# Degree rows gathered into freed edge slots and added to the node sum by an identity product

## The chip, the cores and the metric

The kernel is one program on one core of a Trainium2 chip. A core has five engines with their own instruction streams, which wait for each other by semaphores: TensorE (PE, matrix products into PSUM), VectorE (DVE), ScalarE (ACT), GpSimd (POOL) and SyncE (SP). SP, ACT and POOL also issue transfers, which 16 DMA engines carry out. The metric is the device time of one execution in microseconds (us); less is better.

## The reference

The input is a graph of 6250 nodes with 256 features each and 100000 edges with 128 features each. The layer adds a graph term and a linear attention term to the nodes, and then a mixture of eight experts with two experts per node. What matters here is the graph term:

```python
in_deg  = minimum(segment_sum(ones, dst), 511)
out_deg = minimum(segment_sum(ones, src), 511)
sum3d   = segment_sum(edge_attr @ W_sum + b_sum, src)
gnn     = xn + z_in[in_deg] + z_out[out_deg] + cent_term + vor_term + sum3d
x = x + gnn + mix(xn)                 # xn is the normalised x
x = x + experts(layernorm(x))         # top 2 of 8, H = 1024
```

So each node takes one row of 256 numbers from the table z_in and one from z_out, chosen by its two degrees. Everything is float32.

## The kernel before

Nodes are cut into 49 tiles of 128 (TILES); a tile is 128 partitions by 256 numbers, and all 49 stay in SBUF in the tensor `state`. Edges are cut into 782 columns of 128. The program has these stages.

1. Sorting and side work (to about 1127 us). SP loads edge rows, ten columns at a time, into a ring of five slots (`X`, named `edge_rows` in the profile, 5 x 10 x 129 numbers per partition). POOL writes each column by an indirect DMA to its sorted place in DRAM (`pool_scatter`, L1725). Beside it the other engines count degrees, compute the attention term and the terms of the nodes, and add them to `state` (`vector_rest`, L1288, which counts `rest_added`).
2. Visits. The sorted edges are read back in blocks, and one-hot products sum them for each tile of nodes into `acc`. A batch of four visits is on DVE one subtraction (L1072), one comparison of 128x1024 numbers (L1077) and four additions (L1065), and on PE eight products (L608). The last visits end at about 1243 us. When the scatters are over, the ring of edge slots is free but for four small arrays at its start.
3. Degree rows. After its last scatter POOL runs `pool_z` for steps 0 to 51. Step t issues the gather of z_in for tile t, and the gather of z_out for tile t - 3 (ZLAG). Both are indirect DMAs with `compute_op=ALU.add`: they add the gathered row into `state` itself (`pool_degrees`, L1759). Gather z_in(t) waits for `rest_added`, z_out(t) for the landing of z_in(t), and z_in(t) also for z_out(t - 6), since six semaphores `z_added` go round (ZRING).
4. Node loop (`tensor_nodes`, `vector_nodes`, `scalar_nodes`, 58 ticks), from the end of the visits on. For tile t PE makes `acc` x `wsum` into a PSUM bank (L788). DVE waits for that product (`n_proj`) and for both degree rows (`z_added`), and adds the bank to `state` (L1315, which counts `n_state`). Five tiles behind PE transposes the normalised tile (L780), seven behind it makes the router's logits (L771); DVE has seven more instructions for each tile, ACT four. PE may make product t once tile t - 2 is added, as there are two banks.
5. Routing (from L1341 on) and experts (from L1787 on): gathers of tokens, eight experts' products in float16 in three terms (L830, L844), and scatter-adds into the result (L1798).

Each engine executes its stream in the order that the program gives it, and there is no scheduler. DMAs that POOL issues are one queue.

Of the kernel before, what the change touches and what calls it, by code (L numbers as in the profile page):

```python
# [10 lines left out]
P = 128  # L11
NODES, DIM, EDGES, EDIM = 6250, 256, 100000, 128
# [50 lines left out]
START = 14  # L63
WEVERY = 5
ZRING, ZLAG = 6, 3
BIGN = TILES * DIM + 48

SLOT = 256
# [104 lines left out]
def build_layer(nc, x, src, dst, edge_attr, vor, cent, z_in, z_out, w_cent, b_cent, w_vor, b_vor,  # L173
# [89 lines left out]
    def late(n):  # L263

        late_at[0] += n
        return edge_mem[:, late_at[0] - n:late_at[0]]
# [108 lines left out]
    xh = part(HR * DIM).bitcast(F16).rearrange("p (r i n) -> p r i n", r=HR, i=2)  # L375
    mv2 = late(2 * TILES).rearrange("p (t i) -> p t i", i=2)
    r1, r2 = late(TILES), late(TILES)
    ps_s, ps_y, ps_log = banks[2:4], banks[5:7], banks[7]


# [127 lines left out]
    def x_free(e, n):  # L508

        if n >= XRING:  # L510
            e.wait_ge(scattered[n % XRING], 16 * LOAD * (n // XRING))

    def part_sorted(e, q):

# [251 lines left out]
    def tensor_nodes(e, tick):  # L766
# [16 lines left out]
        if 0 <= t < TILES:  # L783
            if t == 0:
                e.wait_ge(acc_added, VISITS)
            if t >= 2:
                e.wait_ge(n_state, t - 1)
            e.matmul(ps_s[t % 2][:, 0:DIM], acc[:, t * P:(t + 1) * P], wsum, start=True, stop=True).then_inc(n_proj, 1)  # L788

    def tensor_route(e):  # L790
        e.wait_ge(routed, ROUTE_CHOSEN)
# [498 lines left out]
    def vector_nodes(e, tick):  # L1290
# [20 lines left out]
        if 0 <= t < TILES:  # L1311
            st = state[:, t, :]
            e.wait_ge(n_proj, t + 1)
            e.wait_ge(z_added[t % ZRING], 32 * (t // ZRING + 1))
            e.tensor_tensor(st, st, ps_s[t % 2][:, 0:DIM], ALU.add).then_inc(n_state, 1)  # L1315
        t = tick - 4
        if 0 <= t < TILES:
# [436 lines left out]
        for c in range(LOADS * LOAD, ETILES):  # L1754
            pool_scatter(e, c, XL[:, c - LOADS * LOAD, :], scattered[LOADS % XRING], last_row)

    def pool_degrees(e, i, t):
        table = (z_in, z_out)[i]
        e.indirect_dma_start(state[:, t, :], None, table, bass.IndirectOffsetOnAxis(ap=deg_i[:, i, t:t + 1], axis=0),  # L1759
                             bounds_check=DEG - 1, oob_is_err=True, compute_op=ALU.add).then_inc(z_added[t % ZRING], 16)  # L1760

    def pool_z(e, step):
        t = step
        if t < TILES:
            if t == 0:
                e.wait_ge(deg_done, 3)
            e.wait_ge(rest_added, t + 1)
            if t >= ZRING:
                e.wait_ge(z_added[t % ZRING], 32 * (t // ZRING))
            pool_degrees(e, 0, t)  # L1770
        t = step - ZLAG
        if 0 <= t < TILES:
            e.wait_ge(z_added[t % ZRING], 32 * (t // ZRING) + 16)
            pool_degrees(e, 1, t)

    def pool_gather(e, j):
        if j >= BLOCKS:
# [300 lines left out]
```

## Time and profile before

| | us |
|---|---|
| runs, median of 3 | 2031.07 (2030.84 to 2040.11) |
| the profiled execution | 2035.25 |
| its span | 2033.5 |
| PE busy | 1617.6 |
| DVE busy | 1482.0 |
| POOL busy | 1359.2 |
| ACT busy | 672.7 |

The span is the time from the first to the last instruction of the profiled execution. Busy times are sums over the whole span, and the stages above have different limits, so they do not say which engine a stage waits for; that is read from the rows of the stage. An indirect DMA on POOL is busy only while POOL prepares it; the transfer itself comes after, and the view of one line gives the time from issue to landing.

### The profile page before, as it was taken

To read this page: it belongs to the slowest core of one execution; us is meant where nothing else is said; L and a number is where in the kernel's file an instruction comes from. 1 tells how busy PE (TensorE), PEld (TensorE's weight loads), DVE (VectorE), ACT (ScalarE), POOL (GpSimd) and SP (SyncE) were. 2 spreads that over 40 slices of the span, in tenths; PEclk is the share of its full clock that TensorE was granted. 3 is DMA by queue.
4 is the path that set the end of the run, shared out by engine and by line. 5 is a ranking of instruction groups with operands and counts; after the bars stand their busy time and mean duration, and the time that the engine had idled before them with its cause. 6 is when DMAs were issued, how large, how long until landed. Compare 5 with 4: busy or idle time off the path is not lost. (4 is left out here: it accounts for less than half of the span.)

```text
span 2033.5 us, 38723 instructions
## 1 busy us (share of the span) xinstructions
PE 1617.6 (80%) x12552; PEld 1275.3 (63%) x12552; DVE 1482.0 (73%) x3547; ACT 672.7 (33%) x1486; POOL 1359.2 (67%) x1185
## 2 busy tenths in 40 slices
PE   5555543777888887999977777756899999999997
PEld 1121222344555556889876666646798989889896
DVE  6789888866686756666688888879666666666664
ACT  0001111344333434555510003534444344444342
POOL 5778888777777777777777888840354554554442
PEclk9766755798998998999999999657899999999999
DMA  6378777634454545899998996663499999999995
GB/s 184 92 237 248 219 226 221 188 101 130 126 139 124 141 120 140 234 237 237 254 296 242 236 238 123 130 161 114 150 271 266 263 278 271 272 279 274 266 257 152
DMA packets 381288, 413.79 MB, mean 203 GB/s; under 512 B 46438, under 2 KB 297630, under 8 KB 381086
## 3 DMA queue, kind: packets, MB, share of 16 engines
q1 hardware_dynamic: 192328, 192.74, 30.8%
q10 hardware_dynamic: 129462, 126.47, 23.0%
q0 software_dynamic: 59296, 92.09, 18.5%
q8 instruction: 101, 1.65, 0.3%
q14 instruction: 101, 0.83, 0.1%
HBM read 315.53 MB, written 95.62 MB: 202 GB/s over the span
## 5 line engine op out<-in xcount | busy, mean ns | idle before, releaser
L1725 POOL DMA_INDIRECT sorted_rows<-edge_rows,sorted_pos x780 | 851.7, 1092 | 239.1 <-issue 214.1
L1798 POOL DMA_INDIRECT result<-mixw,edge_rows x105 | 169.6, 1615 | 273.3 <-DVE mixw L1475 189.8
L1680 ACT ACTIVATE mixw<-bank,edge_rows 128x256 f32<-128x256 f32 (+1 forms) x456 | 242.4, 549 | 321.4 <-PE bank L830 227.7
L830 PE MATMUL bank<-edge_rows,big 128*128 128x256 f16 (+1 forms) x2736 | 287.8, 264 | 0.0
L844 PE MATMUL bank<-big 128*128 128x256 f16 x2520 | 284.4, 273 | 1.0 <-issue 1.0
L830 PEld LDWEIGHTS bank<-edge_rows,big 128*128 128x128 f16 x2736 | 248.9, 97 | 30.7
L844 PEld LDWEIGHTS bank<-big 128*128 128x128 f16 x2520 | 244.3, 98 | 28.4 <-issue 1.3
L712 PE MATMUL bank<-mixw,xnT 128*128 128x512 f32 x392 | 200.2, 658 | 66.4 <-ACT xnT L1572 66.1
L608 PE MATMUL bank<-big 128*128 128x128 f32 x1680 | 211.6, 280 | 38.0 <-DVE big L1077 38.0
L1065 DVE TENSOR_TENSOR big<-big,bank 128x128 f32 x588 | 168.6, 287 | 84.4 <-PE bank L608 18.5
L608 PEld LDWEIGHTS bank<-big 128*128 128x128 f32 x1680 | 197.7, 193 | 48.0 <-DVE big L1077 47.6
L1787 POOL DMA_INDIRECT state<-xn_rows,edge_rows x105 | 114.3, 1089 | 122.2 <-DVE edge_rows L1434 90.5
L1077 DVE TENSOR_TENSOR big<-iota,big 128x1024 f32<-128x1024 f32 x147 | 180.1, 1225 | 5.1
L712 PEld LDWEIGHTS bank<-mixw,xnT 128*128 128x128 f32 x392 | 77.2, 207 | 154.7 <-issue 81.9
L1461 DVE SCALAR_TENSOR_TENSOR big<-mixw,edge_rows,big 128x512 f16<-128x512 f32 (+1 forms) x228 | 161.8, 710 | 8.1
L1459 DVE TENSOR_SCALAR big<-mixw,edge_rows 128x512 f16<-128x512 f32 (+1 forms) x228 | 106.9, 469 | 64.0 <-ACT mixw L1680 60.1
L1472 DVE SCALAR_TENSOR_TENSOR mixw<-bank,edge_rows 128x256 f32<-128x256 f32 x105 | 50.8, 484 | 119.8 <-PE bank L844 119.6
L1614 ACT ACTIVATE mixw<-mixw,sig_cols 128x128 f32<-128x128 f32 x196 | 80.8, 483 | 89.6 <-issue 56.4
L1759 POOL DMA_INDIRECT state<-L_gnn_z_in,deg_i x49 | 96.3, 1964 | 14.9 <-issue 14.0
L1759 POOL DMA_INDIRECT state<-L_gnn_z_out,deg_i x49 | 94.3, 1924 | 14.9 <-issue 13.7
L587 PE MATMUL bank<-sort_hot,rank_matrix 128*128 128x500 bf16 (+1 forms) x79 | 37.6, 476 | 82.0 <-DVE sort_top L1038 72.2
L608 PE MATMUL bank<-big,mixw 128*128 128x128 f32 x672 | 84.3, 279 | 19.2 <-DVE big L1077 19.2
(328 smaller groups left out, 2631.6 us busy)
## 6 DMA issues: line engine op xcount, KB each, us to landing
big<-w_parts SPq DMA_DIRECT2D x114, 1024.0 KB, 7.1
big<-sorted_rows ACTq DMA_DIRECT2D x420, 129.0 KB
edge_rows<-edge_attr SPq DMA_DIRECT2D x78, 640.0 KB
mixw<-sorted_rows ACTq DMA_DIRECT2D x168, 129.0 KB
big<-L_ffn_W ACTq DMA_DIRECT2D x128, 128.0 KB
w_parts<-big ACTq DMA_DIRECT2D x64, 256.0 KB, 4.3
sorted_rows<-edge_rows,sorted_pos POOLq DMA_INDIRECT x780
edge_rows<-L_ffn_b SPq DMA_DIRECT2D x57, 128.0 KB, 6.4
```

The source lines that it names most:

```text
L608: ins = e.matmul(ps_visit[b % 2][:, i * P:(i + 1) * P], visit_rows[visit_slot(b)[0]][:, i, k, 0:EDIM], visit_hot[:, b % 2, i, k, :], start ...
L712: ins = e.matmul(ps_kv[h], xnT[:, t % 2, k, :], kvw[:, k, h * INNER:(h + 1) * INNER], start=(k == 0), stop=(k == KC - 1))
L830: ins = e.matmul(ps_h[h % 4][:, w], W1r[:, r, a, k, h * P:(h + 1) * P], xT[:, r, b, k, w], start=(k == 0 and s == 0), stop=(k == KC - 1 an ...
L844: ins = e.matmul(ps_o[s][:, 0:DIM], hT[:, r, a, h, s * P:(s + 1) * P], W2r[:, r, b, h, :], start=(h == 0 and i == 0), stop=(h == HC - 1 an ...
L1065: e.tensor_tensor(acc[:, bass.ds(o, P)], acc[:, bass.ds(o, P)], ps_visit[b % 2][:, i * P:(i + 1) * P], ALU.add).then_inc(acc_added, 1)
L1077: e.tensor_tensor(visit_hot[:, b % 2].rearrange("p v k n -> p (v k) n"), iota.unsqueeze(1).to_broadcast([P, n, P]), visit_key[:, b % 2].re ...
L1461: e.scalar_tensor_tensor(lo, hs, m_r[:, n, HC + 1:HC + 2], hi, ALU.mult, ALU.subtract).then_inc(h_parted, 1)
L1680: e.activation(h32[:, h, w], ps_h[h % 4][:, w], ACT.Gelu, bias=m_r[:, n, h:h + 1], scale=m_r[:, n, HC:HC + 1]).then_inc(gelu_done, 1)
L1725: e.indirect_dma_start(sorted_rows, bass.IndirectOffsetOnAxis(ap=row_pos[:, c:c + 1], axis=0), rows, None, bounds_check=last_row, oob_is_e ...
L1759: e.indirect_dma_start(state[:, t, :], None, table, bass.IndirectOffsetOnAxis(ap=deg_i[:, i, t:t + 1], axis=0), bounds_check=DEG - 1, oob_ ...
L1787: e.indirect_dma_start(xg[:, j % XG, h].rearrange("p i k n -> p (i k n)"), None, xn_rows, bass.IndirectOffsetOnAxis(ap=slot_tok[:, s:s + 1 ...
L1798: e.indirect_dma_start(y_rows, bass.IndirectOffsetOnAxis(ap=slot_tok[:, tile:tile + 1], axis=0), yo[:, j % YO, s, :], None, compute_op=ALU ...
```

## The change

The gathers no longer touch `state`. Twenty-four places of 256 numbers (ZROWS) are laid in the ring of edge slots, behind the small arrays that live there (ZAT = 306). z_in(t) is gathered plainly, without an addition, into place (t + 19) mod 24; z_out(t) is gathered with an addition into the same place. PE then adds the place to the node's sum: behind the product with `wsum`, and in the same PSUM accumulation, it multiplies the row with the identity. The wait for the degree rows moves from DVE to PE. z_in(t) no longer waits for `rest_added`; for t below 24 it waits until the edge slots under its place are scattered, from t = 24 on until PE has counted product t - 24, which used the same place.

```diff
+ZROWS = 24
...
+    ZAT = XRING * LOAD * XW - ZROWS * DIM
+    assert late_at[0] <= ZAT
...
+    def z_row(t):
+
+        a = ZAT + (ZROWS - 5 + t) % ZROWS * DIM
+        return edge_mem[:, a:a + DIM]
+
+    def z_slots(t):
+
+        a, w = ZAT + (ZROWS - 5 + t) % ZROWS * DIM, LOAD * XW
+        return range(a // w, (a + DIM - 1) // w + 1)
+
+    def slot_scattered(e, r):
+
+        more = ETILES - LOADS * LOAD if r == LOADS % XRING else 0
+        e.wait_ge(scattered[r], 16 * (LOAD * len(range(r, LOADS, XRING)) + more))
...
@@ tensor_nodes
-            e.matmul(ps_s[t % 2][:, 0:DIM], acc[:, t * P:(t + 1) * P], wsum, start=True, stop=True).then_inc(n_proj, 1)
+            e.matmul(ps_s[t % 2][:, 0:DIM], acc[:, t * P:(t + 1) * P], wsum, start=True, stop=False)
+            e.wait_ge(z_added[t % ZRING], 32 * (t // ZRING + 1))
+            e.matmul(ps_s[t % 2][:, 0:DIM], ident, z_row(t), start=False, stop=True).then_inc(n_proj, 1)
...
@@ vector_nodes
             e.wait_ge(n_proj, t + 1)
-            e.wait_ge(z_added[t % ZRING], 32 * (t // ZRING + 1))
             e.tensor_tensor(st, st, ps_s[t % 2][:, 0:DIM], ALU.add).then_inc(n_state, 1)
...
@@ pool_z
-            e.wait_ge(rest_added, t + 1)
+            if t < ZROWS:
+                for r in z_slots(t):
+                    slot_scattered(e, r)
+            else:
+                e.wait_ge(n_proj, t - ZROWS + 1)
             if t >= ZRING:
                 e.wait_ge(z_added[t % ZRING], 32 * (t // ZRING))
-            pool_degrees(e, 0, t)
+            e.indirect_dma_start(z_row(t), None, z_in, bass.IndirectOffsetOnAxis(ap=deg_i[:, 0, t:t + 1], axis=0),
+                                 bounds_check=DEG - 1, oob_is_err=True).then_inc(z_added[t % ZRING], 16)
         t = step - ZLAG
         if 0 <= t < TILES:
             e.wait_ge(z_added[t % ZRING], 32 * (t // ZRING) + 16)
-            pool_degrees(e, 1, t)
+            e.indirect_dma_start(z_row(t), None, z_out, bass.IndirectOffsetOnAxis(ap=deg_i[:, 1, t:t + 1], axis=0),
+                                 bounds_check=DEG - 1, oob_is_err=True, compute_op=ALU.add).then_inc(z_added[t % ZRING], 16)
```

The order of instructions on POOL is the same; the kind of every other one and its waits change. These rows of POOL's stream, in the degree-row stage, begin with the gather z_in(23) of the kernel before. A row has the line, the operation, what it writes and reads, its size and the semaphores that it waits for:

```order
L1759 DMA state<-L_gnn_z_in,deg_i 128x256 [waits z_added5,rest_added]
L1759 DMA state<-L_gnn_z_out,deg_i 128x256 [waits z_added2]
L1759 DMA state<-L_gnn_z_in,deg_i 128x256 [waits z_added0,rest_added]
L1759 DMA state<-L_gnn_z_out,deg_i 128x256 [waits z_added3]
L1759 DMA state<-L_gnn_z_in,deg_i 128x256 [waits z_added1,rest_added]
```

The same place of POOL's stream in the changed kernel, z_in(23) first:

```order
L1788 DMA edge_rows<-L_gnn_z_in,deg_i 128x256 [waits z_added5,scattered4,scattered3]
L1793 DMA edge_rows<-L_gnn_z_out,deg_i 128x256 [waits z_added2]
L1788 DMA edge_rows<-L_gnn_z_in,deg_i 128x256 [waits z_added0,n_proj]
L1793 DMA edge_rows<-L_gnn_z_out,deg_i 128x256 [waits z_added3]
L1788 DMA edge_rows<-L_gnn_z_in,deg_i 128x256 [waits z_added1,n_proj]
```

The third row is z_in(24), the first gather that reuses a place: it, and the z_out(21) queued behind it, now wait for PE's first node.

On PE one tick of the node loop was, in the kernel before (transposes, product, logits; `mixw` holds the normalised tile, `big` holds `acc`):

```order
L780 MATMUL bank<-ident,mixw 128x128 [waits n_yT,n_y]
L780 MATMUL bank<-ident,mixw 128x128
L788 MATMUL bank<-wsum,big 128x256 [waits n_state]
L771 MATMUL bank<-wr_t,mixw 128x8 [waits n_yT]
L771 MATMUL bank<-wr_t,mixw 128x8
```

In the changed kernel the same tick on PE has one product more, which reads the place in the edge slots:

```order
L798 MATMUL bank<-ident,mixw 128x128 [waits n_yT,n_y]
L798 MATMUL bank<-ident,mixw 128x128
L806 MATMUL bank<-wsum,big 128x256 [waits n_state]
L808 MATMUL bank<-edge_rows,ident 128x256 [waits z_added0]
L789 MATMUL bank<-wr_t,mixw 128x8 [waits n_yT]
L789 MATMUL bank<-wr_t,mixw 128x8
```

The identity product stands between the product and the logits of an older tile, and carries the wait for `z_added` that the addition on DVE had.

## Rows read from the trace of the kernel before

**Rows 1.** Page, chain that ended last: shares of the span by engine.

```profile
PE 31%; POOL 6%; issue 5%; DVE 2%; DMA 2%; POOLq 0%; ACT 0%; DVEq 0%; ACTq 0%
```

**Rows 2.** Line L1759, 1127 to 1244.5 us: count, ns min/median/max, first and last start.

```profile
L1759 POOL DMA_INDIRECT state<-L_gnn_z_in,deg_i x23: 1560/2487/2506, 1127.6 to 1241.4; - x23
L1759 POOL DMA_INDIRECT state<-L_gnn_z_out,deg_i x20: 1560/2487/2487, 1138.1 to 1243.3; - x20
```

**Rows 3.** Line L1759, 1244.9 to 1350 us, with its waits, waiters and landing.

```profile
L1759 POOL DMA_INDIRECT state<-L_gnn_z_out,deg_i x29: 1560/1560/1693, 1247.0 to 1346.1; - x29
L1759 POOL DMA_INDIRECT state<-L_gnn_z_in,deg_i x26: 1560/1560/1653, 1245.1 to 1338.7; - x26
...
  DVE state L1315: 21.2, 11
...
DMA to landing us min/median/max: 3.6/3.9/4.5
```

**Rows 4.** Line L1787 (plain gather, as many bytes a row), 1430 to 1500 us.

```profile
L1787 POOL DMA_INDIRECT state<-xn_rows,edge_rows x19: 1007/1012/1164, 1438.2 to 1490.9; - x19
```

**Rows 5.** Line L1798 (scatter with addition), 1430 to 1500 us.

```profile
L1798 POOL DMA_INDIRECT result<-mixw,edge_rows x8: 1555/1616/1629, 1463.2 to 1498.3; - x8
```

**Rows 6.** Timeline of POOL: start us, us, engine, line, operation [idle before].

```profile
1117.97 0.97 POOL L1725 DMA_INDIRECT sorted_rows<-edge_rows,sorted_pos  x1 [0.30 <-issue]
1119.25 1.21 POOL L1725 DMA_INDIRECT sorted_rows<-edge_rows,sorted_pos  x1 [0.30 <-issue]
...
1140.89 2.49 POOL L1759 DMA_INDIRECT state<-L_gnn_z_in,deg_i  x1 [0.30 <-issue]
1143.68 2.49 POOL L1759 DMA_INDIRECT state<-L_gnn_z_out,deg_i  x1 [0.30 <-issue]
```

**Rows 7.** Timeline of DVE in the visits.

```profile
1118.39 1.23 DVE L1077 TENSOR_TENSOR big<-iota,big 128x1024 f32<-128x1024 f32 x1
...
1121.18 1.23 DVE L1077 TENSOR_TENSOR big<-iota,big 128x1024 f32<-128x1024 f32 x1
...
1140.72 1.23 DVE L1077 TENSOR_TENSOR big<-iota,big 128x1024 f32<-128x1024 f32 x1
```

**Rows 8.** Timeline of PE: the first products, then two neighbours of one tick.

```profile
1243.59 3.47 PE L788 MATMUL bank<-wsum,big 128*128 128x256 f32 x10 [1.82 <-DVE big L1065]
...
1250.38 0.60 PE L788 MATMUL bank<-wsum,big 128*128 128x256 f32 x2
1250.82 0.51 PE L771 MATMUL bank<-wr_t,mixw 128*128 128x8 f32 x4
```

**Rows 9.** Timeline: DVE's additions of tiles 7, 27 and 48, and routing's first.

```profile
1252.41 0.40 DVE L1315 TENSOR_TENSOR state<-state,bank 128x256 f32<-128x256 f32 x1
...
1288.93 0.40 DVE L1315 TENSOR_TENSOR state<-state,bank 128x256 f32<-128x256 f32 x1
...
1350.03 0.40 DVE L1315 TENSOR_TENSOR state<-state,bank 128x256 f32<-128x256 f32 x1
...
1357.99 0.57 DVE L1341 TENSOR_TENSOR mixw<-bank,br_t 128x392 f32<-128x392 f32 x1
```

**Rows 10.** Timeline of PE near the loop's end, granted clock 0.50.

```profile
1347.51 0.67 PE L780 MATMUL bank<-ident,mixw 128*128 128x128 f32 x2
...
1347.97 1.06 PE L788 MATMUL bank<-wsum,big 128*128 128x256 f32 x2
...
1348.82 0.86 PE L771 MATMUL bank<-wr_t,mixw 128*128 128x8 f32 x4
...
1349.53 0.67 PE L780 MATMUL bank<-ident,mixw 128*128 128x128 f32 x2
```

**Rows 11.** Windows: busy us (count) by engine, PEclk, DMA share, GB/s.

```profile
1127.00:1230.00 103.00, 75.62 (x592) 68.57 (x591) 87.18 (x222) 1.28 (x1) 91.65 (x38) 1.00 1.00 238
1244.00:1298.00 54.00, 41.25 (x234) 34.18 (x233) 53.64 (x238) 34.49 (x115) 45.16 (x30) 0.92 0.68 132
1298.00:1350.00 52.00, 33.74 (x129) 29.91 (x128) 30.68 (x129) 19.79 (x64) 41.76 (x27) 0.50 0.62 111
```

More of the change, by code:

```diff
@@ L1755, in pool_last_edges @@
             pool_scatter(e, c, XL[:, c - LOADS * LOAD, :], scattered[LOADS % XRING], last_row)
[L1757 to L1760, printed above, removed]
     def pool_z(e, step):
```

## The prediction

> **What bounds the kernel now.** I read the chain of waits first. By engine it names PE with 31% and POOL with 6% of the span [rows 1]; PE's part is the experts' stage, which the change does not touch, so only the stretch in which POOL is named can move. That is the stretch of the degree rows, and I read POOL's line L1759 there. It starts 43 gathers up to 1244.5 us, 23 of z_in and 20 of z_out [rows 2], and 55 after it, the last at 1346.1 [rows 3]. Between two gathers lie 0.30 us in every timeline row [rows 6], so a gather costs 2.49 + 0.30 = 2.79 us beside the visits and 1.56 + 0.30 = 1.86 us in the node loop: POOL is never free. Then who waits: DVE's addition stands 21.2 us for rows that have not landed [rows 3]. The last addition is at 1350.03, 3.9 us after the last gather's start, which is the time from issue to landing [rows 3, 9]. So POOL's 98 gathers set the end of the node loop, and routing starts 8 us behind it, at 1357.99.
>
> It is not so for the whole loop. From tile 7 to tile 27 DVE takes (1288.93 - 1252.41) / 20 = 1.83 us a tile [rows 9], and it is busy for 53.64 of 54 us [rows 11]: up to about tile 30 DVE is the bound, since POOL had a lead of 20 finished tiles, and POOL only from there, at two gathers or 3.73 us a tile.
>
> **The plain gather.** The trace has no plain gather of these tables. The nearest row is L1787, which gathers 128 rows of the same 1024 bytes without an addition: 1.01 us on POOL [rows 4]. L1798, with an addition, takes at least 1.56 us [rows 5], as L1759 does [rows 3]; the scatter without one takes 0.97 [rows 6]. The addition is what these pairs differ in, so I take 1.01 for z_in. The bounds are 0.97 and 1.56 us. z_out stays at 1.56.
>
> **Beside the visits: almost nothing.** A gather there takes 2.49 us because of DVE's comparison. z_in at 1140.89 starts 0.17 us behind the start of a comparison and ends at 1143.38, which is the comparison's end at 1141.9 plus 1.5 [rows 6, 7]; the next one starts at 1143.68 and meets the next comparison. One gather goes through in each batch of 2.79 us. With one of two at 1.01 us, I place them on that beat: z_in behind a comparison, z_out, z_in again, and only the second z_out starts inside a comparison. That makes four gathers in three batches, 8.4 us for two tiles instead of 11.2. z_in(4) would start at about 1136 and z_in(24) at 1136 + 20 x 4.2 = 1220. But z_in(24) reuses the place of tile 0 and waits for PE's first node, and that cannot be before the last visit: PE's first product starts at 1243.59 [rows 8]. POOL stands about 24 us, with z_out(21) behind it in the queue, and nobody waits for either. So the faster gathers give a lead of 24 and 21 instead of 23 and 20, one tile, and if the beat stays at 2.79 us the lead is just as before. The early start without `rest_added` gives nothing: POOL stands at no wait for it in the first gathers.
>
> The DMA engines show a busy share of 1.00 beside the visits [rows 11], and there will be more rows in that stretch. I cost this at nothing: DVE keeps its 2.79 us there [rows 7], and only two transfers more are issued before the visits end. If visit blocks came late, each microsecond would be one lost.
>
> **In the node loop: the gain.** POOL goes on when PE has done node 0, at 1243.59 + 0.9 = 1244.5. There remain 25 of z_in and 28 of z_out. The last one starts at 1244.5 + 25 x (1.01 + 0.30) + 27 x (1.56 + 0.30) = 1244.5 + 32.8 + 50.2 = 1327.5, against 1346.1: 18.6 us earlier. With z_in at 0.97 it is 19.6, at 1.56 it is 4.9.
>
> DVE must keep up: tile 48 at its own pace is 1252.41 + 41 x 1.83 = 1327.4. The last row lands at 1327.5 + 3.9 = 1331.4, so the rows stay the last by 4 us, from about tile 41 on. If DVE's pace is the end, more of the gathers' gain is useless.
>
> **What PE gets.** 49 identity products of 128x256 float32. The trace has the same shape in L788: 0.60 us alone, and 0.44 from its start to the next instruction's [rows 8]; at half clock 1.06 and 0.85 [rows 10]. At full clock PE is busy 41.25 us for 32 tiles, 1.29 a tile [rows 11], and comes to 1.73, under DVE's 1.83: hidden. At half clock a tile takes 0.46 + 0.85 + 0.71 = 2.02 us by the starts of rows 10, and would take 2.87. In the last stretch, with 3.17 us between rows, that is hidden too, but the last three z_out come 1.86 us apart, so at half clock PE falls behind by 2 x (2.87 - 1.86) = 2.0 us. I take half of that, 1.1. And the last row now passes the identity product before DVE can add it: 0.6 to 1.1 us, I take 1.0. The wait that moved to PE has logits and transposes of older tiles behind it; these were behind DVE's wait too, by way of the normalised tile.
>
> Sum: -18.6 + 1.0 + 1.1 = -16.5 us. Last addition 1333.5; routing and all behind it move as a block, since they start from the last node. The span becomes 2017.0 and the profiled execution's 2035.25 becomes 2018.8. That execution lies 4.2 us above the median of the runs, 2031.07; I forecast against the median: 2014.6 us, written 2014.5.
>
> **Rivals.** *Half clock (the slower side).* The granted clock is full beside the visits, 0.92 on average in 1244 to 1298, and 0.50 from there on [rows 11]. Were it half through the whole loop, PE at 2.87 us a tile would be the bound: 1244.5 + 48 x 2.87 + 1.3 = 1383.6, 33.5 us later than now: 2064.6. It decides from (1350.0 - 1244.5) / 48 = 2.20 us a tile on, which is 17 of 48 tiles at half clock. For it: PE is not quickly back at full clock, 0.50 held to the end. Against it: the same clock stayed full beside the visits with PE busy 75.62 of 103 us, and PE now has a third more to do in each tile. With the 0.92 of before, 8 tiles at half clock cost 8 x 1.04 = 8 us on DVE's 1327.4, that is 4 us net: 2018.5, inside my own range.
> The Trainium skill, page "TensorE: Matmul & The Clock Gate", section "HAM oscillation — how this bites in real kernels", says that a PE which waits for transfers between short pieces of work drops to half clock each time; the rows at 0.50, all in the stretch that waits for degree rows, agree, and by that rule alone half clock belongs to the last tiles, which have room for it.
>
> *The plain gather is no cheaper.* If the 0.55 us belong to the table gather and not to the addition, 25 x 0.55 = 13.8 us are gone and the change gives 2.7: 2028.4. Rows 4 and 5 speak against it, but they are other tensors.
>
> *POOL holds DVE in the visits.* z_out of 1.56 us now sometimes starts before a comparison and runs into it. If the comparison then waited for it, up to 1.2 us in each 8.4 us between 1136 and 1220, the visits would end 10 x 1.2 = 12 us later: 2026.5. Against it: the scatter of 1117.97 ran until 1118.94 over the start of the comparison at 1118.39, and the next comparison still came 2.79 us later [rows 6, 7].
> The Trainium skill, page "SBUF — State Buffer", section "Who interferes with whom", says that whoever starts first keeps the shared port for its whole instruction and that issue order decides who blocks; by it this rival would happen, and also before with the scatters. The trace agrees for POOL behind a comparison and not for DVE behind a scatter, so I go by the rows, with 2014.5 instead of 2026.5.
>
> **How the numbers follow.** My forecast, 2009 to 2021 with the bounds of the gather's price, DVE's pace and some half clock: 0.66. Better than that: 0.04. Half clock in more tiles: 0.17, of which 0.08 ends above 2041. No cheaper gather: 0.08. DVE held: 0.05. The range 2009 to 2030 leaves out the 0.04 below and about 0.12 of the half clock. A measurement can tell about 0.5% from no change, 10.2 us. Faster by more than that, below 2020.9: 0.66 + 0.04 + 0.02 of mild half clock, 0.72. Within: 0.07 of half clock, 0.08 and 0.05, 0.20. Slower: 0.08.
>
> **What would show it.** Right: z_in near 1.01 us in the node loop; a stand of POOL at its 25th z_in until about 1244.5; the last z_out at 1327 to 1328; DVE's last addition at 1332 to 1335; routing about 16 us earlier; comparisons on a beat of 2.79 us. Wrong: z_in at 1.56; PE without a gap at a clock of 0.5 before tile 41; a longer beat in the visits; or a routing stage that takes back what the loop gave.

## The result, and the profile after

The change takes 2017.59 us (median of 5 runs, 2012.65 to 2020.65) where the kernel before took 2035.31 (median of its 5 runs, 2030.84 to 2040.11): a ratio of 0.9912 [0.9895, 0.9929], or 17.7 us less, with an interval of 14.5 to 21.4. The profiled execution took 2020.65 us and its span is 2018.9, against 2035.25 and 2033.5: 14.6 us less in the span. The prediction had 2014.5 us and 16.5 us less.

The page, first the busy time of the engines and then the chain that ended last by engine:

```profile
PE 1623.6 (80%) x12650; PEld 1277.8 (63%) x12650; DVE 1477.1 (73%) x3547; ACT 669.8 (33%) x1486; POOL 1305.3 (65%) x1185
...
PE 49%; DVE 12%; issue 5%; ACTq 5%; ACT 3%; DMA 2%; DVEq 1%; POOL 1%; SPq 0%; POOLq 0%
```

POOL had 6% of the chain [rows 1] and has 1%. (The other shares can't be compared: the shares of [rows 1] add up to 46% of the span and these to 78%, so this chain could be followed further back.) POOL's busy time fell from 1359.2 to 1305.3 us. PE has 98 instructions more, two for each identity product.

The view of the plain gather's line before the node loop, then from 1244.5 us on (count, ns min/median/max, first and last start, then what POOL waited for):

```profile
L1788 POOL DMA_INDIRECT edge_rows<-L_gnn_z_in,deg_i x24: 1012/1031/1967, 1125.9 to 1205.0; - x24
...
L1788 POOL DMA_INDIRECT edge_rows<-L_gnn_z_in,deg_i x25: 1024/1028/1082, 1245.4 to 1322.3; - x25
...
  PE bank L808: 39.3, 10
```

And of the gather with addition, the same two stretches, with its landing in the second:

```profile
L1793 POOL DMA_INDIRECT edge_rows<-L_gnn_z_out,deg_i x21: 1547/1554/2581, 1131.5 to 1207.3; - x21
...
L1793 POOL DMA_INDIRECT edge_rows<-L_gnn_z_out,deg_i x28: 1547/1552/1653, 1246.8 to 1329.2; - x28
...
DMA to landing us min/median/max: 3.6/3.8/4.8
```

These answer to [rows 2, 3]. In the loop z_in costs 1.03 us in place of 1.56, and z_out takes 1.55. The lead at the start of the loop is 24 and 21 gathers instead of 23 and 20, and the last gather starts at 1329.2 instead of 1346.1.

POOL's timeline, a stretch beside the visits and the stand in front of the loop, and then DVE's comparisons in the first stretch:

```profile
1157.48 2.28 POOL L1793 DMA_INDIRECT edge_rows<-L_gnn_z_out,deg_i  x1 [0.30 <-issue]
1160.07 1.96 POOL L1788 DMA_INDIRECT edge_rows<-L_gnn_z_in,deg_i  x1 [0.31 <-DMA edge_rows<-L_gnn_z_out,deg_i]
1162.34 1.55 POOL L1793 DMA_INDIRECT edge_rows<-L_gnn_z_out,deg_i  x1 [0.30 <-issue]
1164.19 1.03 POOL L1788 DMA_INDIRECT edge_rows<-L_gnn_z_in,deg_i  x1 [0.30 <-issue]
1165.52 1.55 POOL L1793 DMA_INDIRECT edge_rows<-L_gnn_z_out,deg_i  x1 [0.30 <-issue]
1167.38 1.03 POOL L1788 DMA_INDIRECT edge_rows<-L_gnn_z_in,deg_i  x1 [0.30 <-DMA edge_rows<-L_gnn_z_out,deg_i]
1168.71 2.28 POOL L1793 DMA_INDIRECT edge_rows<-L_gnn_z_out,deg_i  x1 [0.30 <-issue]
...
1207.28 1.55 POOL L1793 DMA_INDIRECT edge_rows<-L_gnn_z_out,deg_i  x1 [0.31 <-issue]
1245.43 1.03 POOL L1788 DMA_INDIRECT edge_rows<-L_gnn_z_in,deg_i  x1 [36.59 <-PE bank L808]
```

```profile
1157.11 1.22 DVE L1097 TENSOR_TENSOR big<-iota,big 128x1024 f32<-128x1024 f32 x1
1159.90 1.23 DVE L1097 TENSOR_TENSOR big<-iota,big 128x1024 f32<-128x1024 f32 x1
1162.69 1.23 DVE L1097 TENSOR_TENSOR big<-iota,big 128x1024 f32<-128x1024 f32 x1
1165.49 1.29 DVE L1097 TENSOR_TENSOR big<-iota,big 128x1024 f32<-128x1024 f32 x1
1168.35 1.22 DVE L1097 TENSOR_TENSOR big<-iota,big 128x1024 f32<-128x1024 f32 x1
```

The pattern comes back after 11.23 us, from 1157.48 to 1168.71: six gathers, three tiles, in four batches of the visits, 3.74 us a tile where [rows 6] had two batches of 2.79 us. The z_out of 1157.48 starts 0.37 us behind the start of a comparison and takes 2.28 us, the z_in of 1160.07 starts 0.17 us behind one and takes 1.96. The z_out of 1162.34 starts 0.35 us ahead of one, and neither is longer for it. The z_out of 1165.52 starts 0.03 us behind one: it takes its own 1.55 us, and the comparison takes 1.29 us in place of 1.23. Then POOL stands 36.59 us, until PE has counted node 0, although it has work left.

DVE's last additions and routing's first instruction on its timeline, then two of PE's identity products in the stretch at half clock:

```profile
1333.76 0.41 DVE L1334 TENSOR_TENSOR state<-state,bank 128x256 f32<-128x256 f32 x1
...
1341.74 0.57 DVE L1360 TENSOR_TENSOR mixw<-bank,br_t 128x392 f32<-128x392 f32 x1
```

```profile
1314.55 1.22 PE L808 MATMUL bank<-edge_rows,ident 128*128 128x256 f32 x2
...
1317.85 1.22 PE L808 MATMUL bank<-edge_rows,ident 128*128 128x256 f32 x2
```

Against [rows 9] the last addition is 16.27 us earlier and routing 16.25: the block moved as one, up to there. The windows of [rows 11], with the end of the loop at 1334, and a short one inside it (busy us and count by engine, granted clock, DMA share, GB/s):

```profile
1127.00:1230.00 103.00, 75.41 (x589) 68.56 (x590) 87.15 (x223) 1.28 (x1) 68.50 (x44) 1.00 0.93 247
1244.00:1298.00 54.00, 50.91 (x305) 44.20 (x304) 53.30 (x239) 33.42 (x116) 42.54 (x33) 1.00 0.61 140
1298.00:1334.00 36.00, 32.14 (x154) 25.03 (x154) 28.61 (x128) 19.65 (x65) 27.05 (x20) 0.81 0.60 136
1316.00:1322.00 6.00, 5.95 (x19) 4.26 (x19) 3.50 (x16) 2.29 (x8) 5.08 (x4) 0.50 0.58 131
```

Beside the visits DVE is as busy as before, 87.15 us against 87.18. In the first 54 us of the loop PE is busy for 9.7 us more and the clock is full. The half clock that held from 1298 to 1350 is now a piece within 1298 to 1334 (0.50 in the window of 1316). There the identity products come 3.30 us apart, which is the rows' pace and not PE's: [rows 10] and one product more make 2.87 us a tile at this clock, and POOL's timeline in the same stretch has no gap above 0.31 us. (PE shows 5.95 us busy of 6.00 all the same: shown times take in waits. The identity product is shown for 1.22 us here, and for 1.06 at this clock where it doesn't wait, in e0 below.)

```profile
1312.74 1.03 POOL L1788 DMA_INDIRECT edge_rows<-L_gnn_z_in,deg_i  x1 [0.30 <-PE bank L808]
1314.07 1.55 POOL L1793 DMA_INDIRECT edge_rows<-L_gnn_z_out,deg_i  x1 [0.30 <-issue]
1315.93 1.03 POOL L1788 DMA_INDIRECT edge_rows<-L_gnn_z_in,deg_i  x1 [0.30 <-PE bank L808]
```

The gap "until PE bank L808" is the usual one; the product was done before POOL came to it. From 1245.43 on the 53 gathers follow each other without a stand.

### The profile page after: what moved, and what is told of

It reads as the page before. It is cut to its first block, busy times and chain, and to the rows that moved or that the text cites. A ratio compares the mean times of both kernels' runs of the same rounds, so it can differ in the third digit from the quotient of the medians.

```text
span 2018.9 us, 38870 instructions
## 1 busy us (share of the span) xinstructions
PE 1623.6 (80%) x12650; PEld 1277.8 (63%) x12650; DVE 1477.1 (73%) x3547; ACT 669.8 (33%) x1486; POOL 1305.3 (65%) x1185
## 4 chain that ended last, share of the span: by engine, by line
PE 49%; DVE 12%; issue 5%; ACTq 5%; ACT 3%; DMA 2%; DVEq 1%; POOL 1%; SPq 0%; POOLq 0%
PE bank L850 14%; PE bank L864 13%; PE bank L626 6%; PE bank L730 6%; ACTq L1885 3%; DVE big L1097 3%; DVE big L1085 2%; PE bank L764 1%; PE bank L819 1%; PE bank L708 1%; PE bank L821 1%; PE bank L836 1%; PE bank L773 1%; ACT mixw L1633 1%; ACTq L1973 1%
## 5 line engine op out<-in xcount | busy, mean ns | idle before, releaser
L1117 DVE TENSOR_TENSOR hotA<-iotab,dst_h 128x500 bf16<-128x500 bf16 (+1 forms) x79 | 33.0, 417 | 89.4 <-PE bank L641 88.9
L626 PEld LDWEIGHTS bank<-big,mixw 128*128 128x128 f32 x672 | 78.1, 192 | 24.3 <-DVE big L1097 24.3
```

Source lines behind the costliest of these rows:

```text
L626: ins = e.matmul(ps_visit[b % 2][:, i * P:(i + 1) * P], visit_rows[visit_slot(b)[0]][:, i, k, 0:EDIM], visit_hot[:, b % 2, i, k, :], start ...
```

## The experiments

Four chips were used. On the first and the fourth the visits end at about 1243 us. On the second and third they end some 600 us later, and the kernel before takes 2629.26 us (median of 28 runs, 2613.57 to 2645.76) on the second and 2611.9 and 2619.88 (two runs) on the third. So I read, beside the whole time, the **loop**: from DVE's first addition to its last. On the first chip it is 105.7 us before (1244.3 to 1350.0) and 89.1 after (1244.7 to 1333.8), that is 16.6 us less. Where there is only one run of a kernel, only the loop is used. For some I also give the **tail**, from the start of the last z_out to the last addition. It is 3.9 us before and 4.5 after on the first chip.

### Second chip: the change again, the addition back, fewer places, six gathers past the places

**e0_change_again** is the changed kernel with no edit.

> The change itself once more, on the same chip as the others: 0.990 to 0.993 of the kernel before; last addition at 1333 to 1335 us, POOL's stand 35 to 37 us. It is the measure for the two others of which a few microseconds are asked.

Measured: 2637.98 us (12 runs) against 2629.26, ratio 1.0033 [1.0008, 1.0058], so 8.7 us slower where 0.990 to 0.993 was expected. The loop takes 92.3 us (1857.1 to 1949.4). The view of the plain gather's line:

```profile
L1788 POOL DMA_INDIRECT edge_rows<-L_gnn_z_in,deg_i x49: 1015/1032/2054, 1424.4 to 1934.8; - x49
...
  PE bank L808: 358.2, 9
  DVE deg_i L1122: 181.9, 1
```

The degree rows begin at 1424 us, the visits end at about 1857. POOL fills its 24 places and then stands most of 358.2 us in front of the loop. The lead is the same 24 and 21 gathers as on the first chip, however long POOL has. The kernel before has no such limit; what it does with the time was seen on the third chip, below.

The loop is 3.2 us longer than on the first chip, and nearly all of that is the tail: 7.6 us, at a granted clock of 0.50 from about 1923 to 1947. POOL's last z_out, two of PE's products with `wsum` behind it, and DVE's last addition:

```profile
1941.74 1.56 POOL L1793 DMA_INDIRECT edge_rows<-L_gnn_z_out,deg_i  x1 [0.30 <-issue]
...
1942.76 1.06 PE L806 MATMUL bank<-wsum,big 128*128 128x256 f32 x2
...
1945.64 1.06 PE L806 MATMUL bank<-wsum,big 128*128 128x256 f32 x2
...
1949.35 0.40 DVE L1334 TENSOR_TENSOR state<-state,bank 128x256 f32<-128x256 f32 x1
```

At half clock PE takes 2.88 us a tile, and the last rows come 1.87 us apart, so PE falls behind them.

**e1_zin_adds** gives z_in its addition back, in the places. It then adds to what a place still holds, so its sums are not the reference's.

```diff
             e.indirect_dma_start(z_row(t), None, z_in, ...,
-                                 bounds_check=DEG - 1, oob_is_err=True).then_inc(...)
+                                 bounds_check=DEG - 1, oob_is_err=True, compute_op=ALU.add).then_inc(...)
```

> The change with z_in gathered with an addition again, into the same places (the sums are then not the reference's). Theory, the price of the plain gather is the gain: z_in takes 1.56 us on POOL instead of 1.03. POOL still stands at z_in(24) until about 1245.4 us; the last z_out starts at 1245.4 + 25 x 1.86 + 27 x 1.86 = 1342 and DVE's last addition is at 1346 to 1347, 13 us later than in the change (1333.8). Time about 2031, 13 us over the change. Rival, the gain came from the places in the edge ring, the early start or the wait that left DVE: the last addition stays at 1334 and the time near 2017.

Measured: 2650.9 us (9 runs), ratio 1.0082 [1.0053, 1.0111]. z_in takes 1.56 us again:

```profile
L1788 POOL DMA_INDIRECT edge_rows<-L_gnn_z_in,deg_i x49: 1558/1560/2587, 1410.4 to 1936.0; - x49
```

The loop takes 106.5 us, 14.2 more than with the plain gather, and the whole time is 12.9 us more than e0's, as expected. The 25 gathers inside it cost 25 x (1.56 - 1.03) = 13.3 us more. So the addition is what the plain gather saves, and POOL's queue in the loop is where it is saved.

**e2_16_places** lays 16 places instead of 24.

```diff
-ZROWS = 24
+ZROWS = 16
```

> The change with 16 places instead of 24. Theory, the number of places is POOL's lead when the node loop starts, and each place is worth one z_in and one z_out in the loop, 1.33 + 1.86 = 3.19 us: 33 z_in and 36 z_out remain at 1245.4, the last z_out starts at 1245.4 + 33 x 1.33 + 35 x 1.86 = 1354.4, last addition at 1358 to 1359, 25 us later than in the change. Rival, DVE's or PE's pace in the loop sets the end and the lead has slack: last addition at most 3 us later, 1337.

Measured: one run; the loop takes 115.9 us (1851.8 to 1967.7), 23.6 more than with 24 places, or 2.95 us for each place. A tile costs POOL 1.03 + 1.56 + 2 x 0.30 = 3.19 us, so eight tiles of lead are 25.5 us, as expected. The lead at the start of the loop is a term of its own, as large as the price of a gather.

**e4_six_direct** uses the time in which POOL stands: z_in and z_out of tiles 24 to 29 are gather-added into `state`, as in the kernel before, and need no place; the later tiles use places again.

```diff
+ZDIRECT = 6
...
         if 0 <= t < TILES:
             if t < ZROWS: ...
+            elif z_direct(t):
+                e.wait_ge(rest_added, t + 1)
             else:
-                e.wait_ge(n_proj, t - ZROWS + 1)
+                e.wait_ge(n_proj, z_place(t) - ZROWS + 1)
...
-            e.indirect_dma_start(z_row(t), None, z_in, ...)
+            e.indirect_dma_start(z_row(t), None, z_in, ...,
+                                 compute_op=ALU.add if z_direct(t) else ALU.bypass)
```

(`z_row(t)` is `state[:, t, :]` for these six, PE leaves their identity product out, and DVE waits for `z_added` before it adds them.)

> The change, but tiles 24 to 29 take both rows by an addition straight into the state, as before the change, so that POOL uses its stand of 36.6 us for 12 more gathers at 2.79 us; the tiles after them use the 24 places again. Theory, POOL's lead is what holds the end back: the last z_out starts at about 1245.4 + 19 x 1.33 + 21 x 1.86 = 1310, nobody waits for rows any more, and DVE's own pace of 1.75 to 1.83 us a tile sets the last addition at 1253.0 + 41 x 1.78 = 1326 to 1328, 6 to 7 us earlier than in the change. Time 2010 to 2012 where the change has 2017. Rival, PE is already the bound with 1.7 us a tile, or the routing stage takes it back: last addition or time as in the change.

Measured: 2631.11 us (12 runs), ratio 1.0006 [0.9977, 1.0035]; the loop takes 81.6 us. That is 10.7 us less than e0's, where 6 to 7 were expected. (The whole times in the expectation are for a chip like the first.) Its window:

```profile
1861.40:1943.00 81.60, 73.56 (x446) 63.40 (x444) 81.46 (x365) 52.01 (x180) 54.11 (x41) 1.00 0.57 133
```

DVE is busy for 81.46 of 81.60 us: with six tiles more of lead the gathers no longer show, and the loop is DVE's, 1.78 us a tile from tile 7 to tile 27 and 1.74 at the end. The loss on this chip is gone, but nothing is gained on the kernel before.

### Third chip: the kernel before again, no identity product, two of them, all in `state`

**b0_before_again** is the kernel before with no edit.

> The kernel before, once more with a profile, because on the chip of the last runs the sorting and the visits end about 600 us later than in the first profile (node loop from 1857 instead of 1244 us), and the change was 1.0033 of the kernel before there. Theory: POOL's lead decides. With late visits the kernel before has issued all 98 gathers before the loop starts (98 x 2.79 = 273 us, and over 400 us were there), the loop then runs at DVE's pace and takes 82 to 84 us from the first to the last addition, while the change stands at its 24th place and takes 92; that is the 9 us. With early visits, as in the first profile, it takes 105 to 106 us. Rival, the change loses elsewhere (routing, experts, visits): the loop of the kernel before takes over 92 us with late visits too.

Measured: the loop takes 82.2 us (1845.3 to 1927.5), as expected. The view of the gathers' line:

```profile
L1759 POOL DMA_INDIRECT state<-L_gnn_z_in,deg_i x49: 1557/1559/1627, 1405.6 to 1629.1; - x49
L1759 POOL DMA_INDIRECT state<-L_gnn_z_out,deg_i x49: 1560/1831/2589, 1419.9 to 1638.6; - x49
...
  DVE state L1288: 231.6, 20
```

All 98 gathers are out by 1641 us, 204 us before the loop starts, at 1.56 us or more. Here they cost nothing, and the change puts 53 of them back into the loop: 92.3 against 82.2 us, 10.1 more, beside the 8.7 us that the whole time on the second chip shows. (The two loops are from two chips; no chip here ran both kernels with a profile in this schedule.) The wait for `rest_added`, which never held POOL on the first chip, holds it for 231.6 us in 20 gathers here, and costs nothing either.

**e3_no_identity** keeps the gathers as in the change and leaves the identity product out, so the degree rows are missing from the sums; DVE waits for the rows again.

```diff
-            e.matmul(ps_s[t % 2][:, 0:DIM], acc[...], wsum, start=True, stop=False)
-            e.wait_ge(z_added[t % ZRING], 32 * (t // ZRING + 1))
-            e.matmul(ps_s[t % 2][:, 0:DIM], ident, z_row(t), start=False, stop=True).then_inc(n_proj, 1)
+            e.matmul(ps_s[t % 2][:, 0:DIM], acc[...], wsum, start=True, stop=True).then_inc(n_proj, 1)
```

> The change without the identity product; DVE waits for the rows again (the degree rows are then missing from the sums). POOL's stream is that of the change. Theory, the product costs only its own latency behind the last row: the loop from the first to the last addition is 0.5 to 2 us shorter than the change's 89.1 (first chip) or 92.3 (second chip), and the granted clock drops earlier, since PE has less to do. Rival, the product holds the loop up in every tile: at least 4 us shorter.

**e6_identity_twice** makes the identity product twice, which adds the row twice.

```diff
             e.wait_ge(z_added[t % ZRING], 32 * (t // ZRING + 1))
+            e.matmul(ps_s[t % 2][:, 0:DIM], ident, z_row(t), start=False, stop=False)
             e.matmul(ps_s[t % 2][:, 0:DIM], ident, z_row(t), start=False, stop=True).then_inc(n_proj, 1)
```

> The change with the identity product made twice (the degree rows count twice in the sums). Theory, PE has 0.1 us of room in each tile and no more: busy 50.9 of 54 us for 31 tiles is 1.64 a tile, and 0.44 more makes 2.1 against DVE's 1.75 to 1.83, so PE becomes the bound and the loop takes 96 to 102 us instead of 89 to 92. Rival, PE's busy time overstates what it needs, and by its issue times (0.27 + 0.44 x 3 + 0.35 = 1.94 a tile) the loop takes 93 to 95 us; or it is free: 89 to 92.

Measured, loops in the order none, one (the change, second chip), two: 88.5, 92.3, 89.9 us. Their windows, one kernel each:

```profile
1834.30:1922.80 88.50, 74.14 (x359) 62.93 (x358) 81.64 (x365) 52.16 (x179) 69.58 (x53) 0.74 0.63 140
```

```profile
1857.10:1949.40 92.30, 85.71 (x454) 72.42 (x453) 82.41 (x366) 52.61 (x180) 69.63 (x53) 0.87 0.60 135
```

```profile
1839.00:1928.90 89.90, 89.25 (x548) 80.62 (x547) 84.28 (x366) 55.48 (x180) 69.17 (x53) 1.00 0.61 139
```

In all of them POOL's 53 gathers set the pace of the end (69.17 to 69.63 us of busy time and 53 gaps of 0.30). What a product costs is read in the tail: 3.9 us without it, as in the kernel before, and with one 4.5 us (first chip, full clock), 5.6 (the held run on the fourth, below) and 7.6 (second chip, half clock). So one product costs 0.6 to 3.7 us at the end of the loop, and not its 49 x 0.44 = 21.6 us, and how much depends on the granted clock there. That the loop without it is 0.6 to 3.8 us shorter says the same, but across chips and from one run.

With two products the tail is 5.6 us at full clock. What I expected first, a loop of 96 to 102 us, fell, and the last case, 89 to 92 us, held. But the product is not free inside the loop. PE's timeline with two:

```profile
1855.32 0.60 PE L806 MATMUL bank<-wsum,big 128*128 128x256 f32 x2
1855.75 0.59 PE L808 MATMUL bank<-edge_rows,ident 128*128 128x256 f32 x2
1856.19 0.59 PE L809 MATMUL bank<-edge_rows,ident 128*128 128x256 f32 x2
...
1857.23 0.60 PE L806 MATMUL bank<-wsum,big 128*128 128x256 f32 x2
```

PE has no gap and needs 1.91 us a tile, and DVE's additions of tiles 7 to 27 come 1.91 us apart, where they come 1.78 apart with one product and with none. That is the 1.94 us by issue times of the expectation's second case: PE is the bound there. It is hidden because the rows come last: 10.1 us for the first seven tiles and 41 x 1.91 make 88.4 us, just under the measured 89.9. So there was room for one product more, and by this estimate not for two. My error in the first case was to take PE's busy time, 1.64 us a tile at full clock, as what it needs: a product is shown for 0.59 us and the next one starts after 0.43.

The clock in the loop was 0.74, 0.87 and 1.00 with none, one and two, one run each. That the products made the difference is not shown: the kernel of e5, next, has no identity product, and its loop ran at 0.65 here and, with POOL held, at 0.96 on the fourth chip.

**e5_plain_in_state** leaves the places out: z_in is gathered plainly into `state`, over what is there (which is lost, so the sums are not the reference's), and z_out is added to it.

```diff
-            e.indirect_dma_start(z_row(t), None, z_in, ...)
+            e.wait_ge(rest_added, t + 1)
...
+            e.indirect_dma_start(state[:, t, :], None, z_in, ...)
```

> The kernel before with one edit: z_in is gathered plainly into the state, over what stands there (the sums are then not the reference's), z_out is added as before. No places, no identity product. Theory, this has the whole gain of the cheaper gather and no end to the lead: with early visits POOL has about 33 z_in out when the loop starts, the rest ends near 1300 us, and the loop runs at DVE's pace, 82 to 84 us instead of 105.7; z_in takes 1.01 to 1.04 us outside the visits. With late visits, 82 to 84 us as well. Rival, the loop needs the places or PE's addition for its gain: over 88 us.

Measured: the loop takes 85.0 us, 1 above what I expected and 7.3 below the change's on the second chip, with every gather out before it (1394.1 to 1612.7 for z_in, at 1.03 us). It has neither cap nor identity product. It doesn't have all of the clock either, 0.65:

```profile
1829.00:1914.00 85.00, 79.31 (x354) 69.80 (x353) 81.52 (x366) 53.30 (x180) 0.00 (x0) 0.65 0.18 64
```

From about 1848 to 1886, and again from 1895 on, it was 0.50, and the additions of tiles 26 to 30 come 2.03 us apart. That is PE's pace at half clock, 2.02 us a tile by [rows 10]. b0 ran the last 29 us of its loop at 0.50 too, and at 2.03 us a tile. Neither has a gather in its loop. So with the gathers out of the way, PE at half clock is what holds these two loops above DVE's 1.74 to 1.78 us a tile.

### Fourth chip: four kernels with POOL held

All four wait for the same point of the visits before POOL's first z_in. It was meant to give the schedule of the first chip to a chip of any kind.

```diff
             if t == 0:
                 e.wait_ge(deg_done, 3)
+                e.wait_ge(acc_added, VISITS - 168)
```

The fourth chip turned out to be of the early kind (the kernel before: 2034.89 us, 15 runs), so the hold was short, 9.91 us in the first of the four, 3.05 and 3.04 in the next two and none in the last. The runs compare the kernels in one schedule but don't show that the schedule is what differs between chips. The first is the kernel before with the hold, the second the change with it, the third adds ZDIRECT = 6 as above, the fourth is the one with everything in `state`.

> The kernel before with one wait more: POOL may start its first degree gather only when all but 168 of the visits are added, which is 42 batches before the node loop, as it happened by itself in the first profile. It sets the early-visit schedule on any chip. Theory, POOL's lead at the loop's start decides: 23 z_in and 20 z_out are out when the loop starts, and the loop from first to last addition takes 104 to 107 us as in the first profile (105.7), against 82.2 without the hold where visits are late. On such a chip the time is then 21 to 25 us over the kernel before. Rival, what made the loop short there was the chip and not the lead: 82 to 90 us and no change in time.

> The change with the same hold. Theory: it cannot use an earlier start, since its 24 places are full by 1208 of 1244 us in the first profile; so the hold costs nothing, the loop takes 89 to 93 us, and the time is within 2 us of the change without hold. Against the held kernel before it is 13 to 17 us faster, the sign and size of the first chip's result (17.7), although the chip may be another. Rival, the sign belongs to the chip: held, the change is slower than the held kernel before.

> The change with tiles 24 to 29 gathered with additions into the state, and the same hold. Theory: POOL does twelve more gathers at 2.79 us in its stand, the loop is at DVE's pace and takes 81 to 84 us, 6 to 10 us less than the held change; time within 2 us of the kernel before without hold where visits are late, and 21 to 25 us under the held kernel before. Rival, the lead of six tiles is eaten by the slower gathers beside the visits or by waits: over 87 us.

> The kernel before with z_in gathered plainly over the state (its sums are not the reference's), and the same hold. Theory, the cheaper gather alone has the gain, and without places nothing stops the lead: the beat beside the visits is three tiles in four batches, 3.7 us a tile, so about 31 z_in are out when the loop starts, the rest is out some 55 us later, and the loop takes 82 to 85 us. Rival, the places or PE's addition are needed: 95 us or more.

| held kernel | us (runs) | ratio to the kernel before | loop | clock in it |
|---|---|---|---|---|
| before | 2037.97 (10) | 1.001 [0.9989, 1.0031] | 106.2 | 0.59 |
| change | 2023.31 (6) | 0.9938 [0.9918, 0.9958] | 90.2 | 0.91 |
| six direct | 2014.39 (4) | 0.9875 [0.9835, 0.9915] | 80.9 | 1.00 |
| all in `state` | 2010.82 (4) | 0.9877 [0.9833, 0.992] | 80.1 | 0.96 |

The windows of the change and of the third:

```profile
1246.70:1336.90 90.20, 82.97 (x456) 70.32 (x455) 81.66 (x365) 52.84 (x180) 69.55 (x53) 0.91 0.60 138
```

```profile
1250.50:1331.40 80.90, 73.60 (x447) 63.70 (x445) 80.82 (x365) 52.03 (x180) 54.10 (x41) 1.00 0.58 134
```

The change takes 14.7 us off the held kernel before, and 16.0 off its loop, where the first chip had 17.7 and 16.6. Against the kernel before without a hold it is 11.6 us. The six direct tiles take off 8.9 us more and 9.3 of the loop. Twelve gathers of these tiles went out before the loop, so POOL has 41 in the loop's window where it had 53. Those of z_in ran beside the visits at the stretched price, in time that was a stand before:

```profile
L1806 POOL DMA_INDIRECT edge_rows<-L_gnn_z_in,deg_i x43: 1012/1040/1968, 1133.0 to 1309.1; - x43
L1806 POOL DMA_INDIRECT state<-L_gnn_z_in,deg_i x6: 2483/2487/2494, 1216.5 to 1244.4; - x6
```

DVE is busy for 80.82 of 80.90 us. This is the version that beats both kernels: 1.25% under the kernel before on its chip, and 0.44% under the change. (Both were held; the hold made no difference clear of noise to the kernel before, 1.001 [0.9989, 1.0031].) The fourth kernel needs no places and no product, its loop of 80.1 us is 2 us under what I expected, and its time is not clear of the third's, so with the stand filled the gathers have nothing more to give: at 80 us and a clock near full the loop is DVE's, 1.74 to 1.78 us a tile. The kernel with six direct tiles and without the hold was not run on an early chip.

## Why the prediction was right, point by point

**The sum** was -18.6 for the gathers, +1.0 for the product's latency and +1.1 for half clock at the end. Measured in the loop it was -16.9, +0.6 and 0. The mechanism was right and the total of 16.5 us was close partly by luck, as the points on the last z_out and the identity product say. The median came out at 2017.59 and not 2014.5 mostly because the base moved: the kernel before has a median of 2031.07 from three runs and 2035.31 from five.

**The bound** was POOL's gathers in the loop, as read. e1 shows it: 0.53 us on each of 25 gathers gave 14.2 us on the loop.

**The plain gather** at 1.01 us, from a gather of another tensor [rows 4], was 1.03. The rival that it is no cheaper, 2028.4 us, fell.

**Beside the visits** the mechanism was right and two sizes were off. I placed four gathers in three batches, 4.2 us a tile; there were six in four, 3.74 us. In each four batches one z_out starts 0.37 us inside a comparison and takes 2.28 us, and the z_in behind it starts in the next one and takes 1.96; the other four take their own time, though two of them run beside a comparison. I had two stretched gathers in every three batches. z_in(24) was therefore reached at about 1209 instead of 1220, and the stand was 36.6 us, not 24. As the places cap the lead, it changed nothing: one tile of lead, as predicted. What I read wrongly is its worth. "Nobody waits for either" is true of the stand, but e4 and the third held kernel show that the stand holds 9 us of work that could have been done in it.

**POOL holds DVE** (2026.5 us) fell, but not to nothing. In one of four batches a z_out starts 0.03 to 0.04 us behind the comparison, which then takes 1.29 us in place of 1.23, and the next one comes 2.86 us later in place of 2.79. This happened six times, 0.4 us in all: the comparisons ran 0.49 us ahead of those of the kernel before at 1126 us and 0.08 us ahead at 1238. The price I had set for each meeting was 1.2 us. The Trainium skill, page "SBUF — State Buffer", section "Who interferes with whom", says that whoever issues first gets the shared port pair for its whole instruction. It says so of DVE instructions in a mode with two ports; this comparison comes under its line on two inputs in SBUF, and for such instructions the section infers that they don't stop POOL from preparing a DMA. The trace agrees with neither in full. POOL behind a comparison's start does wait: the z_out that starts 0.37 us behind ends 1.43 us after the comparison's end. A gather that starts 0.35 us ahead doesn't hold the comparison (1.23 us), so the measurement decides against the rule in that order.

**The last z_out** was to start at 1327.5 and started at 1329.2. Of the 1.7 us, 0.9 is the later first gather (1245.43, not 1244.5; PE's first product, at 1243.50, was not late) and 25 x 0.02 = 0.5 the price of z_in; the rest is spread over 53 gathers, none of which waited.

**DVE's pace** was taken from before, 1.83 us a tile. It was 1.77: tile 7 was added at 1253.01 and tile 27 at 1288.48. So there was more room beneath the gathers than I had.

**The identity product** was hidden, as predicted. On this chip the 1.1 us for half clock at the end was not needed: the clock was back at full when the last rows came (1.00 from 1328 on), and the last addition is 1333.76, 4.5 us behind the last gather where it was 3.9 [rows 3, 9]. That is 0.6 us, within the 0.6 to 1.1 of the latency alone. The smaller terms cancelled the late z_out: 1333.76 against 1333.5. That the clock came back in time was luck. In e0 it didn't, PE took 2.88 us a tile as I had worked out (2.87), and the tail was 3.7 us over the 3.9, where my two terms are 2.1 together. (Half of the 2.0 us that I had for the falling behind is 1.0, and I wrote 1.1.)

**Half clock as the bound** (2064.6 us) fell: the clock over the loop was 0.71 before and 0.92 after. The argument held against this rival, that PE has a third more to do in each tile, points the right way for this pair; that it is the cause is not shown, as e5 says. The Trainium skill, page "TensorE: Matmul & The Clock Gate", section "HAM oscillation — how this bites in real kernels", says that short pieces of work between waits for transfers drop the clock. The stretch at 0.50 within 1298 to 1334 agrees, where PE's rows come 3.30 us apart. But the prediction says that the rows at 0.50 are all in the stretch that waits for degree rows, and the 0.92 of [rows 11] hides others: 0.61 from 1274 to 1280 and 0.82 from 1280 to 1286, where PE waited for DVE and ACT only, and DVE's first wait for a row is the one before 1303.52. The last 29 us of b0's loop at 0.50 have no gather in them. So waits for transfers are one way to lose the clock here and not the only one.

**Routing and the rest** moved as a block, by 16.25 us. The span fell by 14.6, so 1.6 us of it was given back between routing and the end of this execution, inside the scatter of the runs (2012.65 to 2020.65). Medians give 17.7 us less, the prediction had 16.5.

**What the prediction did not have** is the schedule. It took the place of the degree rows beside the visits as given, and wrote that the early start without `rest_added` gives nothing. On two of four chips they start some 430 us before the loop. There the cap of 24 places is a loss, and the change is slower by 1.0033 [1.0008, 1.0058]. A rival "the cap takes a lead that the old kernel had" could have been worked out from the code and the rows: the change leaves 25 x 1.33 + 28 x 1.86 = 85.3 us of gathers to the loop always, and the kernel before leaves less than that once 98 - 85.3 / 1.86 = 52 gathers are out before it. On the first chip 43 were, on the third all 98.

## What to carry to other kernels

A ring of places between a producer and its consumer sets the largest lead, and the lead at the start of a stage is worth the producer's price for each item (here 3.19 us a tile): count it as a term of its own and ask what it is when the producer comes early. Where a producer stands at a full ring, look for a second place for its results; six of them gave 8.9 us here, on top of the 14.7 of the change. Whether an engine has room for another instruction is read from start to start of its instructions and not from its busy time (0.43 against 0.59 us for a product here), and at the lower clock too: the same product cost 0.6 us at the end of the loop at full clock and up to 3.7 at half.

## What the runs showed of the hardware that was not expected

The same kernel took 2035 us on two chips and 2612 to 2629 on two others. On the second chip DVE's degree step shows waits whose releaser is only "remote", and on the first the same line has none. Of the other two chips the late one has such waits (422.5 us in 45 in the kernel before) and the early one none in this line. The line's view on the second chip, 200 to 1700 us:

```profile
L1117 DVE TENSOR_TENSOR hotA<-iotab,dst_h x79: 211/420/422, 891.4 to 1417.1; 128x500 bf16<-128x500 bf16 x78, 128x100 bf16<-128x100 bf16 x1
...
  remote: 498.9, 48
```

Single stands there last up to 31.3 us. What releases them I could not read from the trace, and the cause is open. No run with the change and the kernel before in both schedules on one chip was made, so that the schedule alone makes the sign of the change is argued from the lead and the places, not shown.

One kernel, z_in gathered plainly into `state`, had a granted clock of 0.65 in its loop on one chip and 0.96 on another, and the loop took 85.0 and 80.1 us. What decides that was not found.

How a gather on POOL and a comparison on DVE disturb each other depends on some hundredths of a microsecond. At 0.35 to 0.38 us ahead of the comparison a z_out costs neither anything. At 0.03 to 0.04 us behind its start the comparison takes 0.07 us more. From 0.08 us behind on it is the gather that waits: it ends 1.43 us after the comparison's end, and a plain z_in 0.9 us after it.
